# Two sets of edits to an eight-core attention and expert layer: where PE adds rows, how skipped steps are counted, and where blocks, products and norms stand

## The reference, cut to what matters

```python
xn = layernorm(x)                      # x: 8 x 2048 x 1024, one batch element on each core
q, k, v = split(xn @ w_qkv.T + b_qkv)  # 16 heads of 64
q, k = silu(q), softmax(k, axis=tokens)
kv = einsum('bhnd,bhne->bhde', k, v);  out = einsum('bhnd,bhde->bhne', q, kv)
out = layernorm(out) * sigmoid((xn @ w_g1.T + b_g1) @ w_g2.T + b_g2)
attn = out @ w_out.T + b_out
# experts: 8 of them, each token goes to 2, at most 769 tokens of a core to one expert
logits = xn @ Wr.T;  w = softmax(top2(logits))
ffn = sum over the token's 2 experts of w * (xn @ We[e])
y = x + attn + ffn
```

## Time and profile before

| what | value |
| --- | --- |
| median of 3 runs (lowest to highest) | 545.15 us (543.25 to 560.69) |
| profiled execution | 543.36 us |
| span of its slowest core, 1 | 541.8 us |
| spans of the other cores | 532.8 to 539.2 us |
| PE busy, share of the span | 463.1 us, 85% |
| DVE, ACT, POOL busy | 289.1, 225.0, 203.5 us |
| chain that ended last | PE 65%, issue 9%, DVE 8%, DMA 6%, ACT 5% |

### The profile page before, as it was taken

How to read it: one execution, slowest core, us unless ns; L and a number is a source line. 1 busy time by engine, 2 the same in 40 slices (tenths; PEclk the granted TensorE clock), 3 DMA queues, 4 the chain that set the end, 5 groups by cost and what they waited for, 6 DMA issues and landing times.

```text
span 541.8 us, 9152 instructions; the slowest of 8 cores (532.8 to 541.8 us)
## 1 busy us (share of the span) xinstructions
PE 463.1 (85%) x3072; PEld 237.3 (44%) x3072; DVE 289.1 (53%) x621; ACT 225.0 (42%) x353; POOL 203.5 (38%) x169
## 2 busy tenths in 40 slices
PE   0778999989979897997977877899999879986996
PEld 0345655544545443543424433444544434432442
DVE  5666552057776661646654664422122424639996
ACT  3497765365455531564535644433433424200000
POOL 2254346000000139331023363345446633349753
PEclk9999999999999999999988999899999979996998
DMA  8898976999407999899898269377379997356995
GB/s 204 262 290 261 203 189 132 140 169 165 78 2 256 344 164 149 97 118 146 97 134 152 67 138 295 85 200 247 117 217 253 232 313 260 141 183 233 318 315 219
DMA packets 38131, 102.73 MB, mean 190 GB/s; under 512 B 4544, under 2 KB 4672, under 8 KB 37888
## 3 DMA queue, kind: packets, MB, share of 16 engines
q0 software_dynamic: 15520, 44.34, 45.0%
q1 hardware_dynamic: 18880, 47.21, 28.2%
q10 hardware_dynamic: 3680, 10.52, 5.4%
HBM read 93.97 MB, written 37.75 MB: 243 GB/s over the span
## 4 chain that ended last, share of the span: by engine, by line
PE 65%; issue 9%; DVE 8%; DMA 6%; ACT 5%; POOL 2%; SPq 2%; DVEq 1%; another core or an unknown queue 0%; ACTq 0%; PEldq 0%; POOLq 0%
PE PS L315 58%; PE PS L319 7%; DMA wlate<-x_tm 3%; ACT stage L323 2%; SPq L79 2%; POOL stage L696 2%; DMA wlate<-wv_t 1%; DVE bst L891 1%; DMA vq<-eo_d 1%; DVE nm L754 1%; ACT vq L323 1%; DMA eo_d<-vq,dtab 1%; ACT stage L330 1%; DVE stage L339 1%; POOL wr L334 1%
## 5 line engine op out<-in xcount | busy, mean ns | idle before, releaser
L315 PE MATMUL PS<-wr,xnt 128*128 128x512 bf16 x512 | 119.6, 391 | 13.7 <-DVE wr L334 7.0
L315 PE MATMUL PS<-xnt,wr 128*128 128x512 bf16 x512 | 119.6, 380 | 0.5 <-ACT vq L323 0.5
L315 PEld LDWEIGHTS PS<-wr,xnt 128*128 128x128 bf16 x512 | 49.8, 100 | 76.0 <-issue 23.1
L315 PE MATMUL PS<-wlate,stage 128*128 128x512 bf16 x288 | 70.9, 398 | 5.0 <-issue 4.8
L315 PEld LDWEIGHTS PS<-xnt,wr 128*128 128x128 bf16 x512 | 47.8, 98 | 51.5 <-issue 3.5
L330 ACT COPY stage<-PS 128x1024 bf16<-128x1024 bf16 x56 | 56.4, 1008 | 16.4 <-PE PS L319 16.2
L334 POOL TENSOR_TENSOR stage<-stage 128x1024 bf16<-128x1024 f32 x16 | 34.2, 2138 | 45.5 <-DVE stage L331 39.8
L315 PE MATMUL PS<-wr,stage 128*128 128x512 bf16 x224 | 50.6, 379 | 0.2 <-issue 0.2
L338 DVE TENSOR_SCALAR vq<-PS,wslot_f 128x512 bf16<-128x512 f32 x24 | 18.0, 750 | 58.6 <-PE PS L315 45.6
L315 PEld LDWEIGHTS PS<-wlate,stage 128*128 128x128 bf16 x288 | 28.0, 101 | 35.9 <-issue 10.2
L994 POOL DMA_INDIRECT eo_d<-vq,dtab x24 | 25.0, 1041 | 48.3 <-ACT vq L323 32.7
(11 more groups left out here) (153 smaller groups left out, 645.4 us busy)
## 6 DMA issues: line engine op xcount, KB each, us to landing
wlate<-x_tm SPq DMA_DIRECT2D x20, 512.0 KB, 6.2
eo_d<-stage SPq DMA_DIRECT2D x4, 2048.0 KB, 15.3
vq<-eo_d SPq DMA_DIRECT2D x16, 512.0 KB, 5.9
xn_d<-stage SPq DMA_DIRECT2D x16, 256.0 KB, 6.6
wlate<-we POOLq DMA_DIRECT2D x2, 2048.0 KB, 34.2
wr<-we POOLq DMA_DIRECT2D x2, 2048.0 KB, 31.1
wb_d<-we POOLq DMA_DIRECT2D x8, 512.0 KB, 18.9
wlate<-wb_d SPq DMA_DIRECT2D x8, 512.0 KB
```

Source lines behind the costliest of these rows:

```text
L315: return PE.run(lambda e: e.matmul(out, l, r, start=start, stop=stop), *toks, sig=sig)
```

## The change

Two sets of edits are put together.

- Counting: each `Lane` gets a second semaphore (`b_pe`, `b_dv` and so on) for steps inside a branch; the Else part waits on that one. A rare tile uses the bank pair and the turn bank that the next tile doesn't use first.
- K stage: `k_trans` and `k_kv` stand one block later, `eT` has 4 buffers, and the first two Q projections (`q_ahead`) stand between the last blocks. Q projections and `g_hidden` take banks 0 and 1 in turn (`q_bank`); `g_hidden` was in bank 6, the gate's.
- `r_hot` is done on DVE in five pieces, over `b` = 0, `u` = 4 to `b` = 1, `u` = 2.
- `a_norm` is split: the small product `a_shift(t)` stays in the odd unit, ACT's `a_norm(t)` comes in the next even unit behind that unit's tanh.
- Output: for tiles 0 and 1 PE adds the second expert row with an identity matmul into the banks (`o_row`), POOL adds it for the others only.

```diff
-        self.count = Count(sem)
+        self.count = self.plain = Count(sem)
+        self.branch = Count(branch)
...
-            for j in range(NJ + 3):
-                if 2 <= j < NJ + 2:
-                    k_trans(j - 2)
+            for j in range(NJ + 4):
+                if 3 <= j < NJ + 3:
+                    k_trans(j - 3)
                 if j < NJ:
                     k_proj(j)
-                if j >= 3:
-                    k_kv(j - 3)
+                if NJ < j < NJ + 3:
+                    q_ahead[j - NJ - 1] = q_mm(0, j - NJ - 1)
+                if j >= 4:
+                    k_kv(j - 4)
...
-                    tk["hot"] = GP.run(lambda e, v=v: e.tensor_tensor(
-                        hot_v[:, :, v, :], hot_c, wide(vals[:, v, :], NJE), ALU.mult),
-                        tk["hc"], tk["vals"])
+                    tk["hot"] = tt(DV, hot_v[:, :, v, :], hot_c, wide(vals[:, v, :], NJE),
+                                   ALU.mult, tk["hc"], tk["vals"])
...
+                    for _ in range({(1, 0): 2, (1, 1): 1, (1, 2): 1}.get((b, u), b == 0 and u < 5)):
                         route.pop(0)()
...
+                    t = 4 * (b - 1) + u // 2
                     if z >= 0:
                         a_gate(z // 8, z % 8)
+                    if u % 2 == 0 and 0 < t <= NT:
+                        a_norm(t - 1)
+                    if z >= 0:
                         a_z(z // 8, z % 8)
                     if b >= NB:
                         m_beside(b - NB, u)
-                    if 1 <= b <= NB:
+                    if 0 <= t < NT:
                         if u % 2 == 0:
-                            a_out(4 * (b - 1) + u // 2)
+                            a_out(t)
                         else:
-                            a_norm(4 * (b - 1) + u // 2)
+                            a_shift(t)
...
-            xtr[J], xgt_tok[J] = m_turn(0 if J <= BESIDE else J % 2, AC, xg[xg_at(J)], xgT[J % 3], xg_tok[J],
+            xtr[J], xgt_tok[J] = m_turn(1 if J == 0 else 0 if J <= BESIDE else J % 2, AC, xg[xg_at(J)], xgT[J % 3], xg_tok[J],
...
-                        pair = (J + 1) % 2 if J < BESIDE else (J + 1) % 3
+                        pair = J % 2 if J < BESIDE else (J + 2) % 3
+                        turn = 0 if J < BESIDE else (J + 1) % 2
...
+            def o_row(t):
+                for h in range(2):
+                    rows_pe[t] = pr_tok[t, h] = mm(
+                        bank[2 * (t % 4) + h], ident[:],
+                        rows_sb[t % 4][:, D + 512 * h:D + 512 * (h + 1)], False, True, r_tok[t],
+                        sig=True)
...
-                a = tt(GP, xb[t], rows[:, D:2 * D], xb[t], ALU.add, r_tok[t], xo_tok[t])
+                a = [r_tok[t], xo_tok[t]]
+                if t >= BY_PE:
+                    a = tt(GP, xb[t], rows[:, D:2 * D], xb[t], ALU.add, *a)
                 r0_tok[t] = tt(DV, xb[t], rows[:, 0:D], xb[t], ALU.add, a)
...
+                if t == 0:
+                    o_sum(t, 0, D)
+                    return o_rows_in(t + 1)
...
-                while added <= t - (2 if t < NT - 2 else 1):
+                while added <= t - (3 if t < 4 else 2 if t < NT - 2 else 1):
```

More of the change, by code:

```diff
@@ L82, in now @@
     def now(self):
-        return (self.count, self.count.n)
+        return [(self.plain, self.plain.n), (self.branch, self.branch.n)]
     def read(self, counts):
@@ L89, in when @@
     def when(self, key, floor):
-        outer, known, made = self.steps, dict(self.passed), self.made
-        self.steps, self.made = [], []
+        outer, known, made, count = self.steps, dict(self.passed), self.made, self.count
+        self.steps, self.made, self.count = [], [], self.branch
         yield
@@ L98, in when @@
         outer.append((("when", key, floor, self.steps, skip), None, 0))
-        self.steps, self.made, self.passed = outer, made + self.made, known
+        self.steps, self.made, self.passed, self.count = outer, made + self.made, known, count
     def play(self, eng, steps=None, vals=None):
@@ L205, in build_nc @@
         ek = sb("ek", [128, 3 * D], BF16)
-        eT = [ek[:, 512 * i:512 * (i + 1)] for i in range(3)]
+        eT = [ek[:, 512 * i:512 * (i + 1)] for i in (0, 1, 2, 5)]
         e_sb = [ek[:, 512 * (3 + i):512 * (4 + i)] for i in range(2)]
@@ L688, in r_spread, with r_hot, f @@
                 return f
-            SPREAD = 5
+            SPREAD = 4 + NV
             for q in range(4):
                 piece(r_spread(8 * q, 8 * q + 8))
-            def r_hot():
-                for v in range(NV):
-                    tk["hot"] = GP.run(lambda e, v=v: e.tensor_tensor(
-                        hot_v[:, :, v, :], hot_c, wide(vals[:, v, :], NJE), ALU.mult),
-                        tk["hc"], tk["vals"])
-            piece(r_hot)
+            def r_hot(v):
+                def f():
+                    tk["hot"] = tt(DV, hot_v[:, :, v, :], hot_c, wide(vals[:, v, :], NJE),
+                                   ALU.mult, tk["hc"], tk["vals"])
+                return f
+            for v in range(NV):
+                piece(r_hot(v))
             def r_table():
@@ L760, in k_exp @@
                 bk = j % 3
-                ex_tok[j] = act(eT[j % 3][:], bank[bk], AF.Exp, nb_tok[j], kv_tr.get(j - 3),
+                ex_tok[j] = act(eT[j % 4][:], bank[bk], AF.Exp, nb_tok[j], kv_tr.get(j - 4),
                                 bias=nb[:, j:j + 1], acc=zs[:, j:j + 1])
@@ L822, in k_final, with q_bank, q_mm @@
                 k_sum.extend([least, weights, most, last])
-            for j in range(NJ + 3):
-                if 2 <= j < NJ + 2:
-                    k_trans(j - 2)
+            q_ahead = {}
+            q_at = {}
+            q_turn = itertools.cycle((0, 1))
+            def q_bank():
+                return next(q_turn)
+            def q_mm(b, oc):
+                bk = q_at[b, oc] = q_bank()
+                for c in range(HC):
+                    p = mm(bank[bk], wv3[2][:, c, 128 * oc:128 * (oc + 1)],
+                           xnT[:, c, 512 * b:512 * (b + 1)], c == 0, c == HC - 1,
+                           t_wq, btok[bk], sig=(c == HC - 1))
+                return p
+            for j in range(NJ + 4):
+                if 3 <= j < NJ + 3:
+                    k_trans(j - 3)
                 if j < NJ:
                     k_proj(j)
-                if j >= 3:
-                    k_kv(j - 3)
+                if NJ < j < NJ + 3:
+                    q_ahead[j - NJ - 1] = q_mm(0, j - NJ - 1)
+                if j >= 4:
+                    k_kv(j - 4)
                 if j < NJ:
@@ L859, in q_proj @@
             def q_proj(b, oc):
-                bk = oc % 2
-                for c in range(HC):
-                    p = mm(bank[bk], wv3[2][:, c, 128 * oc:128 * (oc + 1)],
-                           xnT[:, c, 512 * b:512 * (b + 1)], c == 0, c == HC - 1,
-                           t_wq, btok[bk], sig=(c == HC - 1))
+                p = q_ahead[oc] if b == 0 and oc in q_ahead else q_mm(b, oc)
+                bk = q_at[b, oc]
                 q_tok[b] = btok[bk] = act(qT[b % 2][:, oc, :], bank[bk], AF.Silu, p,
@@ L1040, in m_put, with m_rare @@
                                       *out_tok[J])
-            def m_rare(e, i, pair):
+            def m_rare(e, i, pair, turn):
                 got = fetch_rows(counter(f"c_r{e}_{i}"), xr, e * ET + i, rare_tok.get("tr"),
                                  eo_free[6])
-                rare_tok["tr"], ready = m_turn(0, DV, xr, xrT, got, rare_tok.get("pe"),
+                rare_tok["tr"], ready = m_turn(turn, DV, xr, xrT, got, rare_tok.get("pe"),
                                                eo_free[7])
```

47 lines of the change are left out of this document (30 added, 17 removed).

## The result

| kernel | median of its runs (us) | ratio to the kernel before, 95% interval |
| --- | --- | --- |
| before, same chip | 547.31 | |
| changed | 527.87 (523.26 to 537.59) | 0.966 (0.959 to 0.973) |
| changed, second comparison | 517.61 (before: 546.19) | 0.949 (0.941 to 0.957) |
| changed, third comparison | 523.78 (before: 544.26) | 0.965 (0.960 to 0.970) |

The medians are over all executions; the ratios leave out the slow ones, in which one die's cores lag the other's or the time is over 1.5% above the kernel's shortest. The change gains 3.4% where 5.3% was forecast, and 5.1% and 3.5% in the two later comparisons. The profiled execution took 526.25 us; its slowest core is 2, with a span of 524.7 us, and the eight lie between 513.0 and 524.7. All rows of after are of core 2 unless a core is named.

The account below looks back on a forecast made before the run. PE, busy 85% of the span, was taken as the bound, so its gaps were to go: 6.7 + 2.3 + 14.8 + 2.0 + 1.5 + 2.0 = 29.3 us less, forecast 516 us (5.3% less), range 507 to 528.

Parts of the forecast that it names:

- K stage, start and middle, less the loss at its end: K stage: PE's waits for ACT's exponential go, 6.7 us less, with up to 0.6 us lost at the end.
- table, beyond that: Table: five products on DVE instead of POOL start it earlier, 2.3 us less with the K stage's end loss included.
- tanh, norm, gate, transfers: Stretch to 345 us: norm behind the tanh and new banks remove most of PE's waits, 14.8 us less.
- counting: Experts: five gaps with a fifth tile or at the end shrink, the jump stays, 2.0 us less.
- output: Output stage: PE adds rows, first sum comes early, but DVE's chain limits the gain to 1.5 us.
- clock: After long gaps PE ran at 1.2 GHz; fewer such gaps give 2.0 us less, bounds 0 and 4.8.
- Transfers take the place: Rival, chance 0.13: gathers behind expert 4's weights in POOL's queue come 5 us late for the fourth tile, giving 521.
- a fixed 92: POOL's queue was taken to have 92 us of work from expert 3's load on; gathers land near 276 us, wanted at 278.
- signs of being wrong: Any of: DVE's busy share in the K stage nears 1, PE waits for a gather, a product takes over 2.5 us.
- DVE's case: Rival, chance 0.17: DVE takes the place of the waits in K stage and loop, 13.4 us less gain, giving 529.
- new stall at the K stage's end: K stage's end: PE stands still some 3 us for the first SiLU, behind `mn`, `sbs` and a table load.
- PE's own drain and DVE's Else go from them: Experts, counting term: these parts leave five gaps that sum to 4.1 us, the jump stays; 2.0 us taken.

Follow-up runs that it names:

- the gathers on time: Changed kernel with expert 4's weights loaded in four quarters behind the gathers: ratio 0.940, then 0.952; first turned tile to last gate 54.9 us both times.
- one count: Changed kernel with steps inside a branch counted on the engine's own semaphore again, rare tiles' banks as changed: last gate to end of experts 117.2 us.

## Why the prediction was right or wrong

It was wrong in size: 29.3 us forecast, 19.4 between the medians of the first comparison, 20.5 in the third. The second, with 28.6, is the one in which hardly a core waited for a gather. By stages of the three profiles (means of the medians, less those of before), in its own terms:

| term | forecast | measured | 
| --- | --- | --- |
| K stage, start and middle, less the loss at its end | 6.1 | 6.2 |
| table, beyond that | 2.9 | 0.8 |
| tanh, norm, gate, transfers | 14.8 | 13.0 |
| counting | 2.0 | 1.7, but not by counting |
| output | 1.5 | 2.6 |
| clock | 2.0 | in the rows above |
| sum | 29.3 | 24.3 |

**The step that failed** is the rival "Transfers take the place", which got 0.13 and was left out of the sum. Its mechanism came true to the letter: weights at 249.69, gathers behind them. Its reasoning held too: the queue's work doesn't shrink when PE does. From the issue of expert 3's weights to the landing of expert 4's it took 93 to 98 us before, and 96 to 105 in three profiles of the changed kernel, while PE now wants the tile after some 100. I took a fixed 92, which no row shows (in the profile before it is 96.6 on core 1, and 93 at the least), and a want that left 2 us, held the case to be unlikely on the strength of them, and gave no term to how the queue varies. One of the prediction's own signs of being wrong, that PE waits for a gather, came true. In the first profile the wait costs 3.4 to 5.6 us on six cores, and on core 2 PE's next rows ran at the low clock (7 matmuls in 3.19, 1.01 for turns that take 0.61). With the gathers on time the loop's two stretches give 11.8 + 4.6 = 16.4, which is the 14.8 and most of the clock's 2.0: those waits went about as priced, and PE's waits did not turn into waits for a busy DVE, so DVE's case fell. Against those 54.9 us, the changed kernel's three profiles have 60.7, 56.1 and 58.1: 5.8, 1.2 and 3.2 us at the median is what the failed step cost there, DVE's stalls included.

**The slowest core.** I took core 1 for all. Its head was 105.1 us and it had stalls of its own of 4.8 and 3.0 us. In the profile after, the slowest is core 2, with a head of 111.4, the wait for the gather and DVE's stall: 66.1 us from first turned tile to last gate, where the median has 60.7. Core 1 itself went from 541.8 to 513.0 us, 28.8 less, and that agreement is partly luck, as its own 4.8 us gap went with no edit. The stages from the K stage on give 23.4 in the first profile, by their medians. Most of what lies between that and 19.4 is the head, 1.6 us longer, and the time behind PE's last matmul, 7.8 us at the median and 5.9 before. The slowest core stands further out, too: 4.7 us above the median core before, and 7.0, 7.0 and 7.5 in the three profiles after.

**Table.** A product took 2.02 us (1.9 forecast, though a straight line through its two rows gives 2.0), and PE's wait for the table was 1.6 (1.2). But behind the new stall at the K stage's end PE ran at the low clock: 10.1 to 11.7 us for 40 matmuls instead of 8.8, on 22 of the 24 cores of three profiles. On the two others, with 8.8, the stretch from first K projection to table took 100.9 and 101.0 us and not 102.3 to 103.9. So the clock took 1.4 us and more of this term. I had put that under the clock's term as an offset, and not into the table's. The stall itself was as forecast: 3.0, with `mn`, `sbs` and the table load in a row ahead of the first SiLU.

**Counting.** The step "PE's own drain and DVE's Else go from them" was wrong: 0.74 stays behind a fifth tile that ran, with one count as with two, so it was nearly all the jump. Gaps of 1.22 in mid stage came down to some 0.8, but with one count too, so not by the counting; the banks of the rare tiles, which that run keeps, are the likely cause, and no run has them alone. Behind skipped tiles 0.16 came on. The 1.7 us of the experts are in the kernel with the K stage's edit alone too (116.7), which has no such counting: some cores of the profile before had gaps of their own there.

**Output.** Mis-sized: 1.5 to 3.8 by the medians, and 3 to 5 against the kernel with everything else changed. The mechanism was right: 3.08 for DVE beside POOL and 1.22 alone, the first sum 13.0 us behind the stage's first matmul (456.55 to 469.51) instead of 19.6 (471.16 to 490.74), and the wait of 3.69 ahead of tile 5.

**Page rules.** "TensorE: Matmul & The Clock Gate" of the Trainium skill, in the table at its head, gives PE a queue of 64 instructions, by which the jump would be hidden and 4.1 us gained. The rows disagree: 0.74 us stand behind the branch. What "SBUF — State Buffer" in the Trainium skill says in "Who interferes with whom" was seen again: with two products on POOL, POOL's took 5.0 us each and not 3.2.

**Open.** Why DVE stands still for 4.5 to 10.3 us at the sixth expert tile on up to four cores, and on one before too. It costs PE 2.3 to 8.4 us there. It isn't the place in the stream nor the code beyond the fifth tile. The record of the semaphore narrows it. In 34 of the 46 such stalls of all runs at least four updates of PE's semaphore stand within 0.3 us where DVE goes on, on core 1 of the first profile 6.5 us behind the end of the matmul that DVE needs. The matmuls that they tell of ended over 2.4 us and more, so it looks as if PE had done the work and the news of it came late. What held it wasn't found. Why the queue took 43 us for the weights in one execution and 36 in another isn't settled either.

## What to carry to other kernels

When compute gets faster, list every queue whose work stays the same and compare, on its own clock, when it will be done with when the engine will now want it; where a slack of 2 us was counted on, 12 of 24 cores in three profiles were late by up to 5.6 us. Put what is wanted first ahead in the queue: moving one load behind four gathers gave about 1%. Where the time is that of the slowest of eight cores, make the sum from medians over the cores, and then add what the slowest has beyond them (5 to 7.5 us here). Compare more than once before a term is called wrong: the same program gained 19.4 us in one comparison and 28.6 in another.

## What was not expected of the hardware

- The same load of 2 MB through POOL's queue took 35 to 44 us in the same program in three profiles, and 15 to 18 us when four transfers ahead of it were left out.
- Behind a stall of 3.0 us PE ran at 1.2 GHz for some of the next 10 us, on 22 of 24 cores: 1.3 to 2.9 us more for 40 matmuls.
- Counting a branch's steps apart changed no gap that mattered: 0.74 us behind a branch that ran, with one semaphore or two.
- PE's semaphore updates can be late: on core 1 of the first profile five of them stand within 0.3 us, 4 to 8 us behind the recorded ends of their matmuls, and DVE and ACT stood still until then.
